# Causal mask moved from TensorE's decay products to the products of C and B, and part of the step's small work moved to GpSimd

## The chip, the cores and the metric

One core of a Trainium2 chip runs the whole program in one launch. The metric is the device time of the program in microseconds (us). Engines are named as the profile names them: PE is TensorE, DVE is VectorE, ACT is ScalarE, POOL is GpSimd, SP is SyncE, which here only issues DMA transfers.

## The reference

The input is 8 sequences of 512 tokens with 128 features. A layer norm with modulation is followed by four Mamba-2 layers, a gated residual, a second modulated norm and a feed-forward block with a shared expert and top-2 routing over 8 experts. The change touches only the Mamba-2 layers:

```python
zxbcdt = h @ Wi                                   # z 256, x 256, B 128, C 128, dt 8
xBC = silu(cb + causal 4-tap convolution of xBC)
dt  = softplus(dt + dtb);  A = -exp(Alog);  dA = exp(dt * A)
hs  = hs * dA_t + (dt_t * x_t) * B_t              # state, 8 heads x 32 x 128
y_t = hs @ C_t  + D * x_t
y   = rmsnorm(y * silu(z)) @ Wo
```

## The kernel before

Features lie on partitions and tokens along the free dimension. The recurrence is computed in chunks of 128 tokens, four to a sequence. Within a chunk the output at token t is the sum over s ≤ t of (C_t·B_s) exp(cum_t − cum_s) dt_s x_s, where `cum` is the running sum of dt·A, which is negative. So each chunk needs the 128x128 products of B and C (`bank[5]`, all four chunks side by side), and for each of the 8 heads a 128x128 matrix of decays, with s on partitions and t along the free dimension. For s > t the exponent is positive and the entry has to become zero.

One step handles one sequence of one layer: 32 steps. The steps are software-pipelined over three steps: the body of step k does part A of step k (projection, convolution, step size), part B of step k−1 (decays, products, state) and part C of step k−2 (norm and output projection); N marks that step k+1 exists. The middle steps are a hardware loop. Every engine has its own program order, written out by hand, and all ordering between engines is by counting semaphores. A wait holds all that stands behind it on that engine.

Names that the prediction uses:
- `tap(t, s)` on DVE: the four taps of the convolution of feature block t (0 and 1 are x, 2 is B, 3 is C). `tap(0, 0)` opens the step on DVE. The blocks are read straight from PSUM banks 0 and 1, so `project(t)` on PE, which fills bank t mod 2, waits for the last tap of block t−2. `project(4)` and `project(5)` make z.
- `decays(n)` on PE, n = 0 to 3: two banks (2 and 3) of four heads each, for a pair of chunks. For each bank there is a mask matmul (identity x mask, 128 rows, 512 columns), one matmul with `PC` as weights and the negative selection `nselb` moving (32 rows, 512 columns), which gives −cum_s, and four of 128 columns with `selb` as weights and `PC` moving, which give +cum_t, the positive half. That is 12 matmuls per call and 48 per step.
- `decay_exp(i)` on ACT: E = exp of a decay bank, i = 0 to 7. `apply_decay(i)` on DVE: M = E x products of C and B, written M0 to M7 in the prediction. `within(c)` on PE: the 8 heads of chunk c, needs M of its chunk. M5 overwrites a tile that `within(1)` reads, and so waits for it.
- `softplus` (the tile `dt_`), `running_sum` (`cum`), `decay_to_end` (`wdec`) and `scale_out` (`o_sb`) on DVE. `dA` on ACT is made from `dt_`.
- `p0`, `p1`, `p2` on POOL: `cum` split in three bf16 parts, rows 0 to 23 of each group of 32 partitions (one group for each chunk). SP copies p2 to `PC` (one DMA) and to `P4` (three), which PE reads in the next step.
- `rows_of_heads` on PE and `E2`, `ti` on ACT and DVE: the part of the output that comes from the state before the chunk.
- `ms` in the prediction is the 512-column matmul of `mean128` and `sqh` (line 604). It uses bank 0 again, and waits for ACT to copy z's first half out of it (`zraw`, line 1022). The second half is copied at line 1047. Both go through Silu later in the step, when ACT has loaded the Silu table.

Weights of the feed-forward block are split on POOL and stored by SP during steps 1 to 18; that is the `W` in the bodies of both.

Of the kernel before, what the change touches and what calls it, by code (L numbers as in the profile page):

```python
# [60 lines left out]
def build(nc, x, w_in, w_out, par, cst, c_t, wmod, par2, w1, w2, out):  # L61
    ctx = ExitStack()
    with ctx:
# [323 lines left out]
        def _(pe):  # L387
# [68 lines left out]
            def body(k, A, B, C, N):  # L456
# [1308 lines left out]
```

## Time and profile before

| | us |
|---|---|
| median of 3 runs | 1203.54 (1201.79 to 1203.59) |
| profiled execution | 1201.13 |
| its span in the trace | 1199.3 |
| PE busy | 1056.5 (88%) |
| DVE busy | 1001.3 (83%) |
| ACT busy | 889.5 (74%) |
| POOL busy | 578.0 (48%) |

The profiled execution is 2.4 us below the median of the runs, and 1.8 us longer than its span. The steps of the Mamba-2 layers fill the span from about 31 us to about 850 us. In the middle of it (400 to 700 us) the granted TensorE clock is 1.00, and of 300 us PE is busy 289.71, DVE 270.83, ACT 263.26 and POOL 151.71.

### The profile page before, as it was taken

The page shows a single profiled execution, that of the slowest core. Times are in us where ns is not written, and L with a number is a line of the kernel's source. Part 1 is how long each engine was busy: PE and PEld are TensorE (multiplying, and loading weights), DVE is VectorE, ACT ScalarE, POOL GpSimd, SP SyncE. Part 2 cuts the span into 40 slices and gives each one's busy share as a digit, 9 for nine tenths or more (in the row PEclk, how much of TensorE's full clock was granted, in tenths as well). Part 3 has the DMA queues.
Part 4 walks back from the last instruction along what each step waited for, and adds up shares of the span by engine and source line. Part 5 has one row for each costly group of instructions (what it writes and reads, how often), then busy time and mean ns, then how long its engine had stood idle before and what let it go on. Part 6 is the DMA issues. An engine that isn't in the chain of part 4 may idle for free.

```text
span 1199.3 us, 27505 instructions
## 1 busy us (share of the span) xinstructions
PE 1056.5 (88%) x7160; PEld 603.5 (50%) x7160; DVE 1001.3 (83%) x1864; ACT 889.5 (74%) x1724; POOL 578.0 (48%) x721
## 2 busy tenths in 40 slices
PE   5699999999999999999999999997688876999980
PEld 4245544455445554455445554444344444777760
DVE  6798999999998999888998899885578875888865
ACT  5688888888888888888888888886466543565540
POOL 0254566446654566435543455434245451566661
PEclk9899999999999999999999999999789987999995
DMA  4111422233222322210000100000010014776737
GB/s 137 36 34 34 144 91 83 83 115 122 84 85 85 136 98 85 75 29 23 22 22 24 29 19 24 22 16 1 3 33 32 27 36 142 233 227 219 233 117 210
DMA packets 85581, 98.08 MB, mean 82 GB/s; under 512 B 20698, under 2 KB 65888, under 8 KB 85536
## 3 DMA queue, kind: packets, MB, share of 16 engines
q1 hardware_dynamic: 80544, 89.08, 23.5%
q0 software_dynamic: 4992, 8.48, 2.1%
q8 instruction: 18, 0.29, 0.1%
q14 instruction: 27, 0.22, 0.1%
HBM read 59.67 MB, written 37.83 MB: 81 GB/s over the span
## 4 chain that ended last, share of the span: by engine, by line
PE 53%; DVE 20%; issue 13%; ACT 8%; DVEq 2%; DMA 1%; POOL 1%; SPq 1%; ACTq 0%; POOLq 0%
PE bank L475 8%; PE bank L548 5%; ACT xbc L1062 4%; DVE cv L1331 4%; PE bank L604 3%; PE bank L522 3%; PE bank L667 3%; DVE cv L1327 3%; PE bank L484 2%; PE bank L485 2%; PE bank L492 2%; PE bank L491 2%; DVE stmp L1434 2%; DVE M L1341 2%; PE bank L668 2%
## 5 line engine op out<-in xcount | busy, mean ns | idle before, releaser
L1331 DVE SCALAR_TENSOR_TENSOR cv<-bank,PAR,cv 128x511 f32<-128x511 f32 (+2 forms) x384 | 273.8, 740 | 9.1 <-DVE cv L1327 4.2
L1637 POOL TENSOR_TENSOR yt<-yt,ti 128x384 f32<-128x384 f32 x64 | 64.2, 1004 | 331.0 <-DVE ti L1453 331.0
L1341 DVE TENSOR_TENSOR M<-E,bank 128x512 f32<-128x512 f32 x256 | 170.6, 677 | 38.8 <-PE bank L548 30.9
L929 ACT ACTIVATE E<-bank 128x512 f32<-128x512 f32 x256 | 148.6, 594 | 28.1 <-DVE M L1341 27.6
L475 PE MATMUL bank<-hn,WA 128*128 128x512 f32 x256 | 144.6, 647 | 21.0 <-DVE cv L1331 20.6
L1668 POOL DMA_INDIRECT RS<-y,XR x92 | 99.6, 1083 | 78.1 <-DVE y L1546 56.4
L1079 ACT ACTIVATE hr<-bank,W1B 128x512 f32<-128x512 f32 x92 | 63.3, 688 | 57.1 <-PE bank L669 53.4
L1661 POOL DMA_INDIRECT XS<-stage,IDX x64 | 64.5, 1008 | 79.5 <-DVE run L1306 55.7
L1062 ACT ACTIVATE xbc<-cv 128x512 f32<-128x512 f32 x128 | 77.0, 626 | 21.7 <-DVE yt L1448 20.5
L1641 POOL TENSOR_TENSOR y<-yt,zs 128x512 f32<-128x512 f32 x64 | 81.3, 1271 | 20.6 <-POOL yt L1637 19.9
L548 PE MATMUL bank<-M,dtx 128*32 128x128 f32 x2048 | 82.5, 278 | 9.9 <-DVE M L1341 7.3
L1476 DVE TENSOR_TENSOR hL<-hr,hH 128x512 fp32r<-128x512 f32 x124 | 87.2, 703 | 4.3
L1601 POOL TENSOR_TENSOR dtx<-xtok,DTW 128x256 f32<-128x256 f32 x128 | 82.0, 641 | 16.8 <-ACT xtok L949 16.8
L522 PE MATMUL bank<-maskb,idb 128*128 128x512 bf16 x256 | 81.3, 383 | 1.7 <-DMA P<-p 1.7
L548 PEld LDWEIGHTS bank<-M,dtx 128*32 128x32 f32 x2048 | 49.1, 109 | 55.1 <-issue 50.6
L1474 DVE CAST hH<-hr 128x512 fp32r<-128x512 f32 x124 | 54.1, 436 | 25.2 <-ACT hr L1079 22.5
L475 PEld LDWEIGHTS bank<-hn,WA 128*128 128x128 f32 x256 | 39.1, 191 | 65.4 <-issue 46.7
L653 PE MATMUL bank<-hn,WA 128*128 128x512 f32 x128 | 63.4, 618 | 0.6 <-ACT DTW L1051 0.6
L1327 DVE TENSOR_SCALAR cv<-bank,PAR 128x512 f32<-128x512 f32 x64 | 51.6, 806 | 13.6 <-ACT xbc L1062 13.5
L1606 POOL TENSOR_TENSOR xw<-xtok,DTW 128x256 f32<-128x256 f32 x96 | 60.6, 631 | 0.0
L644 PEld LDWEIGHTS bank<-xbc,S 128*128 128x128 f32 x384 | 47.6, 192 | 17.8 <-DVE S L1440 13.6
L508 PE MATMUL bank<-CST,xbc 128*128 128x128 f32 x384 | 54.2, 277 | 2.3 <-ACT u L958 0.5
(242 smaller groups left out, 2657.5 us busy)
## 6 DMA issues: line engine op xcount, KB each, us to landing
XS<-PADT SPq DMA_DIRECT2D x32, 520.0 KB, 4.0
WA<-w_in SPq DMA_DIRECT2D x192, 64.0 KB, 1.8
W1B<-WD SPq DMA_DIRECT2D x23, 514.0 KB, 3.5
W2B<-WD SPq DMA_DIRECT2D x23, 512.5 KB, 4.9
WD<-WS SPq DMA_DIRECT2D x16, 512.0 KB, 2.7
XR<-XS SPq DMA_DIRECT2D x23, 260.0 KB, 4.4
RW<-w_in SPq DMA_DIRECT2D x18, 256.0 KB, 4.3
WO_raw<-w_out SPq DMA_DIRECT2D x32, 128.0 KB, 3.5
```

The costliest lines, as they stand in the source:

```text
L475: mm(bank[t % 2][:, :], WA[t][:, :], hn[:, :], start=True, stop=True).then_inc(pj_mm, 1)
L522: mm(bank[2 + b][:, :].rearrange("p (n t) -> p n t", n=4), idb[:, :], maskb[:, :].unsqueeze(1).to_broadcast([P, 4, P]), start=True, stop=F ...
L548: ins = mm(bank[6 + hh // 4][q:q + 32, c * CH:(c + 1) * CH], dtx[c][:, hh * HD:(hh + 1) * HD], M[2 * (hh // 4) + c % 2][:, (hh % 4) * CH:( ...
L929: f(E[i % 2][:, :], bank[2 + i % 2][:, :], ACT.Exp).then_inc(e_a, 1)
L1062: f(xbc[t][:, :], cv[t][:, :], ACT.Silu).then_inc(silu_a, 1)
L1327: ts(cv[t][:, :], src[:, :], PAR[:, bass.ds(cw + 3, 1)], PAR[:, bass.ds(pk + C_CB + t, 1)], ALU.mult, ALU.add).then_inc(tap_v[t], 1)
L1331: stt(out=cv[t][:, s:L], in0=src[:, 0:L - s], scalar=PAR[:, bass.ds(cw + 3 - s, 1)], in1=cv[t][:, s:L], op0=ALU.mult, op1=ALU.add).then_in ...
L1341: tt(M[i % 4][:, :].rearrange("p (n t) -> p n t", n=4), E[i % 2][:, :].rearrange("p (n t) -> p n t", n=4), bank[5][:, c * CH:(c + 1) * CH] ...
L1476: tt(hL[t][:, :], hr[t][:, :], hH[t][:, :].bitcast(F32), ALU.subtract).then_inc(hl_v, 1)
L1601: tt(dtx[c][:, :].rearrange("p (h d) -> p h d", h=NH), xv, DTW[:, 32 * c:32 * c + NH].unsqueeze(2).to_broadcast([P, NH, HD]), ALU.mult).th ...
L1641: tt(y2[t][:, :], yt[t][:, :], zs[:, bass.ds((j % 2) * 2 * L + t * L, L)], ALU.mult).then_inc(fin_p, 1)
L1668: nc.gpsimd.indirect_dma_start(RS[:, :], bass.IndirectOffsetOnAxis(ap=XR[i % XD][:, (c + 1) * ROW - 1:(c + 1) * ROW].bitcast(I32), axis=0) ...
```

## The change

1. `decays(n)` loses the mask matmul. Rows 24 to 31 of each group of 32, which were empty, now carry a coarse mask: in `PC` row 24 + b is one for the tokens of the b-th block of 16, and in `nselb` it is −1e30 for the columns of all earlier blocks of 16. They are made once at the start, from an iota on POOL. So the matmul with `nselb` also sends whole blocks before the token's own to −1e30, and only inside the 16x16 blocks on the diagonal positive exponents are left. SP must not write over these rows: it copies 24 rows of each group in four DMAs, where it copied 128 rows in one.
2. The four 128-column matmuls with `selb` as weights are replaced by one matmul of 512 columns for each bank: weights are ones (32 rows), the moving operand is `own`, a block-diagonal copy of p2 (p2 x `selb`, 128x1024 bf16) that POOL makes in two instructions. So `decays(n)` has 4 matmuls of 512 columns, 16 per step.
3. On DVE a new instruction `causal_products` multiplies the four chunks of products in `bank[5]` by a 0/1 table in place (PSUM in, PSUM out). M0 waits for it. `apply_decay` becomes min(E, 1) x products in one scalar_tensor_tensor with an immediate.
4. `dt_` and `wdec` move from DVE to POOL: `dt_` is the first thing of POOL's body, `wdec` stands behind p2.
5. ACT no longer copies z's second half. Its Silu reads bank 1 directly, and stands first after the Silu table load; `project_early(k + 1, 1)` on PE waits for it in place of the copy.

```diff
-SILU_TURN = [3, 4, 0, 5]
+SILU_TURN = [3, 4, 1, 5]
@@ SP
-                    sp.dma_start(PC[:, :], p2[:, :]).then_inc(p4_in, 16)
+                    if not B:
+                        wait(sp, const_v, 10)
+                    for c in range(NC):
+                        q = 32 * c
+                        sp.dma_start(PC[q:q + 24, :], p2[q:q + 24, :]).then_inc(p4_in, 16)
@@ PE, decays(n)
-                                wait(pe, p4_in, 64 * (j + 1))
+                                wait(pe, p4_in, 112 * (j + 1))
                             wait(pe, fin_v, 4 * j - 1 + b)
-                        mm(bank[2 + b][:, :].rearrange("p (n t) -> p n t", n=4), idb[:, :],
-                           maskb[:, :].unsqueeze(1).to_broadcast([P, 4, P]), start=True, stop=False)
+                        q = 32 * (pair + b)
+                        mm(bank[2 + b][:, :], PC[q:q + 32, :], nselb[q:q + 32, g * 512:(g + 1) * 512],
+                           start=True, stop=False, tile_position=(q, 0))
                     for b in range(2):
                         q = 32 * (pair + b)
-                        mm(bank[2 + b][:, :], PC[q:q + 32, :], nselb[q:q + 32, g * 512:(g + 1) * 512],
-                           start=False, stop=False, tile_position=(q, 0))
-                    for n4 in range(4):
-                        hh = 4 * g + n4
-                        for b in range(2):
-                            q = 32 * (pair + b)
-                            ins = mm(bank[2 + b][:, n4 * P:(n4 + 1) * P], selb[q:q + 32, hh * P:(hh + 1) * P],
-                                     PC[q:q + 32, :], start=False, stop=(n4 == 3), tile_position=(q, 0))
-                            if n4 == 3:
-                                ins.then_inc(d_mm, 1)
+                        if n == 0 and b == 0:
+                            wait(pe, own_p, 2 * (j + 1))
+                        mm(bank[2 + b][:, :], onesb[q:q + 32, :], own[q:q + 32, g * 512:(g + 1) * 512],
+                           start=False, stop=True, tile_position=(q, 0)).then_inc(d_mm, 1)
@@ PE, before the early projection of the next step's second block
-                    wait(pe, zc_a, 2 * k + 2)
+                    wait(pe, silu_a, 6 * k + 1)
@@ ACT
-                    wait(act, dtc_v, 4 * k + 1)
+                    wait(act, step_p, 2 * k + 1)
                     f(dA[:, :], dt_[:, :], ACT.Copy, scale=PAR[:, bass.ds(pk + C_NA, 1)]).then_inc(da_a, 1)
...
-                    wait(act, pj_mm, 6 * k + 6)
-                    f(zraw[1][:, :], bank[1][:, :], ACT.Copy).then_inc(zc_a, 1)
...
+                    wait(act, pj_mm, 6 * k + 6)
+                    wait(act, fin_p, 4 * (k - 1))
+                    f(zs[:, bass.ds((k % 2) * 2 * L + L, L)], bank[1][:, :], ACT.Silu).then_inc(silu_a, 1)
                     silu(TB)
@@ DVE
+                def causal_products():
+
+                    g = bank[5][:, :].rearrange("p (c t) -> p c t", c=NC)
+                    wait(dve, g_mm, j + 1)
+                    tt(g, g, causal[:, :].unsqueeze(1).to_broadcast([P, NC, CH]), ALU.mult).then_inc(g_v, 1)
+
...
-                        wait(dve, g_mm, j + 1)
+                        wait(dve, g_v, j + 1)
                     wait(dve, y_mm, 4 * j + c - 1)
-                    tt(M[i % 4][:, :].rearrange("p (n t) -> p n t", n=4),
-                       E[i % 2][:, :].rearrange("p (n t) -> p n t", n=4),
-                       bank[5][:, c * CH:(c + 1) * CH].unsqueeze(1).to_broadcast([P, 4, CH]),
-                       ALU.mult).then_inc(m_v, 1)
+                    stt(out=M[i % 4][:, :].rearrange("p (n t) -> p n t", n=4),
+                        in0=E[i % 2][:, :].rearrange("p (n t) -> p n t", n=4), scalar=1.0,
+                        in1=bank[5][:, c * CH:(c + 1) * CH].unsqueeze(1).to_broadcast([P, 4, CH]),
+                        op0=ALU.min, op1=ALU.mult).then_inc(m_v, 1)
@@ DVE, once at the start
+            dve.wait_ge(below_p, NC)
+            ts(ex[:, :], u[:, :], 0.0, -1e30, ALU.is_lt, ALU.mult).then_inc(const_v, 1)
+            dve.wait_ge(const_v, 7)
+            stt(out=nselb[:, :].rearrange("p (h t) -> p h t", h=NH), in0=CST[:, K_SEL:K_SEL + 1024].rearrange("p (h t) -> p h t", h=NH),
+                scalar=-1.0, in1=ex[:, :].unsqueeze(1).to_broadcast([P, NH, P]), op0=ALU.mult, op1=ALU.add).then_inc(const_v, 1)
+            ts(PC[:, :], u[:, :], 0.0, None, ALU.is_equal).then_inc(const_v, 1)
@@ POOL
+                if A:
+                    wait(pool, dta_a, 5 * k + 3)
+                    wait(pool, tr_mm, k)
+                    tt(dt_[:, :], u[:, :], ln1[:, :], ALU.add).then_inc(step_p, 1)
...
+                    wait(pool, dta_a, 5 * k + 4)
+                    tt(wdec[:, :], dt_[:, :], ecs[:, :], ALU.mult).then_inc(step_p, 1)
+                def own_rows(g):
+
+                    if B:
+                        wait(pool, d_mm, 8 * k)
+                    wait(pool, part_p, 4 * k + 4)
+                    tt(own[:, g * 512:(g + 1) * 512].rearrange("p (h t) -> p h t", h=4), p2[:, :].unsqueeze(1).to_broadcast([P, 4, CH]),
+                       selb[:, g * 512:(g + 1) * 512].rearrange("p (h t) -> p h t", h=4), ALU.mult).then_inc(own_p, 1)
```

On DVE, in the loop body, the stretch from the last taps of the first blocks to the running sum (`L1327`, `L1331` taps; `L1351` is `dt_`; `M` is a call of `apply_decay`) reads before:

```order
L1331 SCALAR_TENSOR_TENSOR cv<-bank,PAR,cv 128x510
L58 ISA
L58 ISA [waits g_mm,e_a]
L1341 TENSOR_TENSOR M<-E,bank 128x512 [waits y_mm]
L58 ISA
L1351 TENSOR_TENSOR dt_<-u,ln 128x128 [waits tr_mm,dta_a]
L58 REGISTER_ALU
L1341 TENSOR_TENSOR M<-E,bank 128x512 [waits y_mm,e_a]
L1331 ISA [waits tap1_v]
L1331 SCALAR_TENSOR_TENSOR cv<-bank,PAR,cv 128x509
L58 REGISTER_ALU
L1355 SCALAR_TENSOR_TENSOR cum<-ones_row,dA 128x128 [waits da_a]
```

and now (`L1338` is `causal_products`, `L1347` is `apply_decay`):

```order
L1331 ISA [waits tap1_v]
L1331 SCALAR_TENSOR_TENSOR cv<-bank,PAR,cv 128x510
L1338 TENSOR_TENSOR bank<-bank,causal 128x512 [waits g_mm]
L58 ISA
L58 ISA [waits g_v,e_a]
L1347 SCALAR_TENSOR_TENSOR M<-E,bank 128x512 [waits y_mm]
L58 REGISTER_ALU
L1347 SCALAR_TENSOR_TENSOR M<-E,bank 128x512 [waits y_mm,e_a]
L1331 ISA [waits tap1_v]
L1331 SCALAR_TENSOR_TENSOR cv<-bank,PAR,cv 128x509
L58 REGISTER_ALU
L1356 SCALAR_TENSOR_TENSOR cum<-ones_row,dA 128x128 [waits da_a]
```

The causal product stands in front of M0, and `dt_` between M0 and M1 is gone. `wdec`, further down in front of `spend`, is gone too.

On PE, `decays(3)` and what stands behind it reads before (`L604` is `ms`, `L548` is `within(1)`):

```order
L575 MATMUL bank<-P,selxb 128x384 [waits e2_a]
L58 REGISTER_ALU
L522 MATMUL bank<-maskb,idb 128x512 [waits e_a]
L58 REGISTER_ALU
L522 MATMUL bank<-maskb,idb 128x512 [waits e_a]
L526 MATMUL bank<-nselb,PC 128x512 x2
L532 MATMUL bank<-PC,selb 128x128 x8
L58 REGISTER_ALU
L58 ISA [waits sqh_a]
L604 MATMUL bank<-sqh,mean 128x512 [waits zc_a]
L58 REGISTER_ALU [waits m_v]
L548 MATMUL bank<-M,dtx 32x128 [waits px_p]
```

and now (`L529` is `nselb`, `L535` is `own`, `L605` is `ms`):

```order
L576 MATMUL bank<-P,selxb 128x384 [waits e2_a]
L58 REGISTER_ALU
L529 MATMUL bank<-nselb,PC 128x512 [waits e_a]
L58 REGISTER_ALU
L529 MATMUL bank<-nselb,PC 128x512 [waits e_a]
L535 MATMUL bank<-own,onesb 128x512 x2
L58 REGISTER_ALU
L605 MATMUL bank<-sqh,mean 128x512 [waits zc_a,sqh_a]
L58 REGISTER_ALU [waits m_v]
L549 MATMUL bank<-M,dtx 32x128 [waits px_p]
```

Twelve matmuls are now four, with the same waits ahead of them.

On SP, the end of the step's transfers reads before (`L319` is `PC`, `L321` is `P4`):

```order
L58 ISA [waits d_mm]
L319 DMA PC<-p 128x128 [waits part_p]
L321 DMA P<-p 32x128 x3
L58 REGISTER_ALU
L325 ISA [waits split_p]
L325 DMA WD<-WS 128x1024
```

and now:

```order
L58 ISA [waits d_mm]
L325 DMA PC<-p 24x128 [waits part_p]
L325 DMA PC<-p 24x128 x3
L327 DMA P<-p 32x128 x3
L58 REGISTER_ALU
L331 ISA [waits split_p]
L331 DMA WD<-WS 128x1024
```

Three DMA issues more stand ahead of the three to `P4` and of all later ones.

## Rows read from the trace of the kernel before

**Rows 1.** Waits, 100 to 800 us: engine, line <- releaser: total us, times, longest.

```profile
ACT dA L983 <- DVE dt_ L1351: 25.8, 29, 1.0
DVE M L1341 <- PE bank L548: 25.1, 28, 1.1
```

**Rows 2.** Timeline of DVE: start, us, engine, line, operation, tiles, count, [idle before].

```profile
419.28 0.75 DVE L1331 SCALAR_TENSOR_TENSOR cv<-bank,PAR,cv 128x511 f32<-128x511 f32 x1 [0.15 <-DVE cv L1327]
...
420.67 2.71 DVE L1331 SCALAR_TENSOR_TENSOR cv<-bank,PAR,cv 128x510 f32<-128x510 f32 x4
...
423.89 0.61 DVE L1351 TENSOR_TENSOR dt_<-u,ln 128x128 f32<-128x128 f32 x1
424.42 0.67 DVE L1341 TENSOR_TENSOR M<-E,bank 128x512 f32<-128x512 f32 x1
425.02 0.73 DVE L1331 SCALAR_TENSOR_TENSOR cv<-bank,PAR,cv 128x509 f32<-128x509 f32 x1
...
428.95 0.69 DVE L1369 TENSOR_TENSOR o_sb<-bank,rY 128x512 f32<-128x512 f32 x1
429.55 2.29 DVE L1331 SCALAR_TENSOR_TENSOR cv<-bank,PAR,cv 128x509 f32<-128x509 f32 x3
...
434.58 2.10 DVE L1341 TENSOR_TENSOR M<-E,bank 128x512 f32<-128x512 f32 x3 [0.70 <-PE bank L548]
...
448.48 0.62 DVE L1351 TENSOR_TENSOR dt_<-u,ln 128x128 f32<-128x128 f32 x1
```

**Rows 3.** Timeline of PE in the same step.

```profile
425.90 1.10 PE L475 MATMUL bank<-hn,WA 128*128 128x512 f32 x2
...
430.44 1.10 PE L475 MATMUL bank<-hn,WA 128*128 128x512 f32 x2
...
438.63 1.98 PE L653 MATMUL bank<-hn,WA 128*128 128x512 f32 x4
...
442.25 0.75 PE L522 MATMUL bank<-maskb,idb 128*128 128x512 bf16 x2
```

**Rows 4.** Timeline of PE, decays(3) between its neighbours.

```profile
431.73 0.60 PE L522 MATMUL bank<-maskb,idb 128*128 128x512 bf16 x2
432.27 0.39 PE L526 MATMUL bank<-nselb,PC 32*128 32x512 bf16 x2
432.50 0.39 PE L532 MATMUL bank<-PC,selb 32*128 32x128 bf16 x8
432.81 0.70 PE L604 MATMUL bank<-sqh,mean 128*128 128x512 f32 x1
```

**Rows 5.** Timeline of ACT in the same step.

```profile
431.57 0.60 ACT L1022 ACTIVATE zraw<-bank 128x512 f32<-128x512 f32 x1 [0.33 <-PE bank L475]
...
437.28 1.28 ACT L1062 ACT_TABLE_LOAD   x1
```

**Rows 6.** Groups by line and form: operation, tiles, shapes, count, busy us, mean ns.

```profile
L1341 DVE TENSOR_TENSOR M<-E,bank 128x512 f32<-128x512 f32 x256 | 170.6, 677 | 38.8 <-PE bank L548 30.9 <-PE bank L559 2.4 <-ACT E L929 1.5
...
L1331 DVE SCALAR_TENSOR_TENSOR cv<-bank,PAR,cv 128x511 f32<-128x511 f32 x128 | 95.0, 742 | 4.8 <-DVE cv L1327 4.2 <-ACT cv L941 0.2
```

**Rows 7.** The same for two small DVE forms.

```profile
L1522 DVE TENSOR_TENSOR st<-tile_no,st 128x23 f32<-128x23 f32 x1 | 0.2, 183 | 0.0
L1524 DVE SCALAR_TENSOR_TENSOR row_f<-ee,st 128x23 f32<-128x23 f32 x1 | 0.2, 183 | 0.0
```

**Rows 8.** The same for POOL.

```profile
L1628 POOL TENSOR_TENSOR WS<-RW,WS 128x512 fp32r<-128x512 f32 x16 | 20.5, 1280 | 1.3
...
L1614 POOL TENSOR_TENSOR r<-cum,p 128x128 f32<-128x128 f32 x32 | 13.7, 427 | 2.5
```

**Rows 9.** Timeline of SP, DMA issues at the end of the step.

```profile
436.28 0.53 SPq L319 DMA_DIRECT2D PC<-p  x1
436.85 1.86 SPq L321 DMA_DIRECT2D P<-p  x3
```

**Rows 10.** DMA issues by line: KB each, median us from issue to landing.

```profile
P<-p SPq DMA_DIRECT2D x96, 8.0 KB, 1.7
```

More of the change, by code:

```diff
@@ L83, in build @@
         mean256 = sb("mean256", P)
-        idb, onesb = sb("idb", P, BF16), sb("onesb", P, BF16)
-        maskb = sb("maskb", P, BF16)
+        onesb = sb("onesb", P, BF16)
+        causal = sb("causal", P)
         selb = sb("selb", 1024, BF16)
@@ L116, in build @@
         nselb = sb("nselb", 1024, BF16)
+        own = sb("own", 1024, BF16)
         WA = [sb(f"WA{t}", P) for t in range(6)]
@@ L122, in build @@
         xbc = [sb(f"xbc{t}", L) for t in range(4)]
-        zraw = [sb(f"zraw{t}", L) for t in range(2)]
+        zraw = sb("zraw", 2 * L)[:, 0:L]
         u, ax, ex, ln1 = sb("u", P), sb("ax", P), sb("ex", P), sb("ln1", P)
@@ L602, in body @@
                     wait(pe, sqh_a, k + 2)
-                    wait(pe, zc_a, 2 * k + 1)
+                    wait(pe, zc_a, k + 1)
                     mm(bank[0][:, :], mean128[:, :], sqh[:, :], start=True, stop=True).then_inc(ms_mm, 1)
                 elif A:
-                    wait(pe, zc_a, 2 * k + 1)
+                    wait(pe, zc_a, k + 1)
                     square_mean_of_h(0)
@@ L611, in body @@
                     project(5)
-                    wait(pe, dtc_v, 4 * k + 4)
+                    wait(pe, dtc_v, 2 * k + 2)
+                    wait(pe, step_p, 2 * k + 2)
                     if N:
@@ L1004, in body @@
                 if A:
-                    wait(act, dtc_v, 4 * k + 2)
+                    wait(act, dtc_v, 2 * k + 1)
                     f(ecs[:, :], cum[:, :], ACT.Exp, scale=-1.0, bias=cum[:, CH - 1:CH]).then_inc(dta_a, 1)
@@ L1021, in body @@
                     wait(act, pj_mm, 6 * k + 5)
-                    f(zraw[0][:, :], bank[0][:, :], ACT.Copy).then_inc(zc_a, 1)
+                    f(zraw[:, :], bank[0][:, :], ACT.Copy).then_inc(zc_a, 1)
                 if B:
@@ L1062, in silu @@
                         f(xbc[t][:, :], cv[t][:, :], ACT.Silu).then_inc(silu_a, 1)
+                    wait(act, pj_mm, 6 * k + 6)
+                    wait(act, fin_p, 4 * (k - 1))
+                    f(zs[:, bass.ds((k % 2) * 2 * L + L, L)], bank[1][:, :], ACT.Silu).then_inc(silu_a, 1)
                     silu(TB)
-                    for t in range(2):
-                        if t == 0:
-                            wait(act, zc_a, 2 * k + 2)
-                        wait(act, fin_p, 4 * (k - 1))
-                        f(zs[:, bass.ds((k % 2) * 2 * L + t * L, L)], zraw[t][:, :], ACT.Silu).then_inc(silu_a, 1)
+                    wait(act, zc_a, k + 1)
+                    f(zs[:, bass.ds((k % 2) * 2 * L, L)], zraw[:, :], ACT.Silu).then_inc(silu_a, 1)
                     silu(X0)
@@ L1355, in running_sum @@
                     nc.vector.tensor_tensor_scan(cum[:, :], ones_row[:, :], dA[:, :], 0.0, ALU.mult, ALU.add).then_inc(dtc_v, 1)
-                def decay_to_end():
-                    wait(dve, dta_a, 5 * k + 4)
-                    tt(wdec[:, :], dt_[:, :], ecs[:, :], ALU.mult).then_inc(dtc_v, 1)
                 def chunk_decay():
@@ L1463, in _ @@
             dve.wait_ge(s_cst, 16)
[L1464 to L1465 removed]
+            ts(causal[:, :], CST[:, K_MASK:K_MASK + P], 0.0, None, ALU.is_ge).then_inc(const_v, 1)
             cp(selb[:, :], CST[:, K_SEL:K_SEL + 1024]).then_inc(const_v, 1)
[L1467 removed]
+            dve.wait_ge(below_p, NC)
[4 more added lines that the diff above has]
+            ts(PC[:, :], u[:, :], 0.0, None, ALU.is_equal).then_inc(const_v, 1)
             cp(selxb[:, :], CST[:, K_SELX:K_SELX + 256]).then_inc(const_v, 1)
@@ L1586, in _ @@
             tt = nc.gpsimd.tensor_tensor
+            for c in range(NC):
+                nc.gpsimd.iota(u[32 * c:32 * c + 32, :], pattern=[[1, 8], [0, 16]], base=24, channel_multiplier=-1,
+                               allow_small_or_imprecise_dtypes=True).then_inc(below_p, 1)
+                pool.wait_ge(below_p, c + 1)
             nc.gpsimd.memset(PADT[:, :], 0.0).then_inc(padt_p, 1)
@@ L1609, in body @@
                 if A:
-                    wait(pool, dtc_v, 4 * k + 2)
+                    wait(pool, dtc_v, 2 * k + 1)
                     tt(p0[:, :], cum[:, :], CST[:, K_M1:K_M1 + 1].to_broadcast([P, CH]), ALU.mult).then_inc(part_p, 1)
@@ L1632, in body @@
                     tt(hb, hb, o_sb[:, :], ALU.add).then_inc(hup, 1)
+                if A:
+                    own_rows(0)
+                    own_rows(1)
                 if B:
@@ L1638, in body @@
                         wait(pool, fin_p, 4 * j + 1 + 2 * t)
-                        wait(pool, silu_a, 6 * j + 2 + t)
+                        wait(pool, silu_a, 6 * j + 3)
                         wait(pool, out_mm, j)
```

18 lines of the change are left out of this document (5 added, 13 removed).

## The prediction, made before the changed kernel was run

> **What bounds the kernel now.** The table of busy times comes first: PE 88%, DVE 83%, ACT 74%, and none of them at its limit. In such a kernel a saving counts only if it lies on the path through the step, so the rest is read from one step of the loop. The waits of the middle of the run come second [rows 1]: 28 times, once a step, M5 on DVE waits for `within(1)` on PE, 25.1 us in all, 0.90 us a time; ACT's `dA` waits for `dt_`, 25.8 us in 29 times, 0.89 us a time. Third, the timelines. The period is 448.48 − 423.89 = 24.59 us [rows 2], and 30 steps run at it.
>
> Which of PE and DVE leads changes within a step. From M5 (434.58) through the state update to the fourth of the first taps (420.67 in the next step, that is 445.26) DVE works without a gap that another engine causes. After that the two hand over to each other. `tap(1, 3)` starts at 425.02 and lasts 0.73; `project(3)` starts on PE at 425.90 [rows 2, 3]. The output projection behind it ends just before `o_sb`, 428.95. `tap(2, 3)` starts at 429.55, 0.74 us for one of the three, and ends at 430.29 by that; `project(4)` starts at 430.44 [rows 2, 3]. Then PE alone: `rows_of_heads`, `decays(3)` 431.73 to 432.81, `ms`, `within(1)`, and M5 starts when it ends [rows 4, 2]. So of the four calls of `decays`, only the one behind `project(4)` is on the path. The others end before a DVE result that PE needs anyway.
>
> **decays(n) on PE.** From the start of the mask pair to `ms` it takes 432.81 − 431.73 = 1.08: the mask pair 0.54, the `nselb` pair 0.23, the eight small ones with what follows 0.31 [rows 4]. A single `nselb` matmul of 512 columns would take about half the mask pair's time, so the two with different row groups run side by side. The new call is two such pairs, 2 x 0.23, and a tail of 0.10 (0.31 less four overlapped pairs of 128 columns at a quarter of 0.21): 0.56, or 0.67 if the first pair also pays the 0.11 by which the mask pair exceeds two times 0.215. I take 0.60 and a saving of 0.48; bounds are 0.41 and 0.54, and zero if the pairs did not overlap (4 x 0.27 = 1.08). Times four that is 1.9 us of PE a step, of which 0.48 is on the path.
>
> **The causal product on DVE.** The trace has no DVE instruction that writes PSUM. The nearest rows are M, 677 ns for 512 elements with one PSUM input, and the tap, 742 ns [rows 6]; a write to PSUM could cost something more, and from below the spacing of back-to-back M is 0.60. I take 0.69, between the two rows and like `o_sb` [rows 2]. M0 reads its result, and such a wait between neighbours on DVE costs 0.15 beyond the end of the first [first of rows 2]. So M0 starts 0.84 later. `dt_` gives back its spacing, 424.42 − 423.89 = 0.53 [rows 2]. Everything from `tap(1, 3)` on is 0.31 later on DVE.
>
> **apply_decay with a clamp.** Does scalar_tensor_tensor cost the 65 ns more that separate the tap from M [rows 6]? The tap has a pointer to a scalar in SBUF; the clamp's scalar is an immediate. Two small forms tell them apart: 183 ns for tensor_tensor and 183 ns for scalar_tensor_tensor with an immediate at 23 elements [rows 7]. I take nothing; the other bound is 8 x 0.065 = 0.52 a step, of which four stand ahead of `o_sb`.
>
> **dt_ and wdec to POOL.** A 128x128 tensor_tensor of POOL is 427 ns [rows 8]. `dt_` comes before `dtx`, at once after the last product of the step before, and is ready for `dA` by about 1.0 us earlier; ACT's wait of 0.89 goes. ACT then runs into its next wait: E2 needs M0, which is later by 0.84. So the ACT gain is spent before it reaches `cum` or the output norm, and I count it as nothing. `wdec` stands behind p2 and is needed some 5 us later. Off DVE it leaves only more idle time before M5, since M5 waits for PE.
>
> At 128x128 `dt_` is 0.61 on DVE [rows 2], much more than 128 elements explain. The Trainium skill (SBUF — State Buffer, "Who interferes with whom") says that a VectorE instruction with two SBUF inputs contends with a GpSimd instruction that reads SBUF, and one with at most one SBUF input does not. By that rule the causal product, with one input in PSUM, pays no such price although POOL works beside it. If it paid what `dt_` pays over the 0.23 or so that its size asks for, 0.38, the gain per step would be gone; no row here shows a multiply into PSUM beside POOL.
>
> **own on POOL.** Two instructions of 128x512 with two inputs, 1.28 each at most by the nearest row [rows 8], 2.6 together. They wait for the last decays of the step (432.5), and in steps with weights at most one instruction of that size, the addition to `h`, may still stand before them then: they end by 436.5. PE needs them at 441.9, and POOL had nothing to do from that addition to `ti`. They cost nothing, and would not at twice the price. The Trainium skill (GPSIMD Engine Reference, "3. Performance versus the Vector engine") has GpSimd at about half of VectorE's rate for two inputs and keeps elementwise work on VectorE; the rate agrees with the row (1280 ns against 692 for `o_sb`), and the rule would speak against the change only if POOL were on the path.
>
> **PC in four transfers.** An issue on SP takes 0.53 and 0.62 [rows 9]; three more are 1.9 us. Before, the last of `P4` is issued at 436.85 + 1.24 = 438.09 and lands at 439.8 [rows 9, 10]; PE asks for it in `decays(0)` at 442.25 [rows 3]. Now SP begins 0.33 earlier (below), at 435.95, issues seven at 0.62, the last at 439.67, and it lands at 441.4; PE asks at 441.9. This hides, with 0.5 us to spare, and the `decays(0)` that is shorter by 0.48 gives as much again before PE is late for the transposes behind it. Cost nothing.
>
> **z's second half.** ACT loses a copy of 0.5 us between `rB` and the copy to `DTW`. The table load starts at 437.28 [rows 5], now about 0.8 earlier, and Silu of bank 1 ends near 438.4. PE's early projections start at 438.63 [rows 3] with the other bank first and reach bank 1 near 439.3. The new wait costs nothing in steady state. ACT's Silu of x waits for DVE's `yt` as before, so the earlier table load gains nothing.
>
> **The sum.** `tap(1, 3)` is 0.31 later. `project(3)` had 425.90 − 425.75 = 0.15 in hand, of which some 0.06 is the signal: it moves by 0.23, and `o_sb` behind it. `tap(2, 3)` then ends at 430.52, and `project(4)` starts at 430.58: 0.14 to 0.15 later. `decays(3)` gives 0.48: `ms` at 432.48 in place of 432.81. The other input of `ms` is the `zraw` copy, 431.57 + 0.60 [rows 5], which shifts with `project(4)` to end at 432.32, so `ms` can't be before 432.38. M5 is 0.33 earlier (0.43 at most). From M5 to the next first taps all is as it was. Gain 0.33 a step, or with c for the causal product's duration: 1.02 − c. 30 steps give 9.9 us. Outside them I take 1 us of loss, about half of the three more issues (1.9 us) for which the first `decays(0)`, right behind its transfers, may have to wait. 1201.13 − 9.9 + 1.0 = 1192.2 for the profiled execution, and 2.4 more for the median: **1194.6 us**.
>
> **Rivals.**
> - *More than this.* If the pairs start under `rows_of_heads` and the causal product costs its spacing alone (0.60), the whole wait of M5 comes into reach: 0.5 to 0.9 a step, 1178 to 1190. For: 0.90 of slack on DVE. Against: the copy of `zraw`, which caps `ms`. 0.10.
> - *No change: the clamp at the tap's price.* Four of 65 ns before `o_sb` take 0.26 of the 0.33, and three more behind M5 another 0.13. That leaves −0.06: 1206. Against it stand the equal small forms. At half that price 0.13 a step is left, 1200.6. Together, 1200 to 1206, 0.15.
> - *Slower: the multiply in place.* If reading and writing PSUM take turns, c is twice 0.68, 1.36. 1.02 − c gives −0.34 a step, 1214.7. It decides from c = 0.99, and is a loss of over 2.4 us from 1.07. For: no row excludes it, and DVE leads where it stands. 0.10.
> - *The transfers are late.* With 0.2 us more for each of seven issues `decays(0)` is 0.9 us late, of which 0.48 is covered: 0.42 a step, against 0.33 gained, 1207. For: four of the seven are of a size that the trace does not show. Against: the 0.5 us in hand. 0.05.
> - *Forecast*, 0.60: c from 0.60 to 0.80 and a `decays` saving from 0.41 to 0.54 give 0.15 to 0.42 a step, 1191.6 to 1200.
>
> The range is 1186 to 1204: it adds the part of the first two rivals nearest to the forecast. A change of less than 0.2%, 2.4 us, can't be told from none with this kernel. Faster takes the forecast, the first rival and part of the others: 0.77. Same 0.11, slower 0.12.
>
> **What would show it.** In the changed profile: the causal product in its own group, near 0.69 us; `apply_decay` at 677 ns; `decays(3)` from start to `ms` about 0.6; the wait of M5 for `within(1)` shorter than 0.9 but there; no wait of `dA` for `dt_`; a period of 24.26. PE should wait more, for `tap(1, 3)` and `tap(2, 3)`. Wrong would be: a causal product above 1 us, `decays(0)` waiting for `P<-p` in each step, or M5 without any wait.

## The result, and the profile after

The changed kernel takes 1198.78 us (median of 10 runs, 1196.68 to 1200.79). The kernel before took 1201.41 in its 10 runs beside them (1199.65 to 1203.92). The ratio is 0.9973, 95% interval 0.9963 to 0.9983: 2.6 us or 0.27% faster. The prediction was 1194.6, 8.9 us below the median of before. The direction holds; the gain is three tenths of the one forecast.

The profiled execution took 1199.3, its span 1197.3. Busy time per engine, the first part of the page:

```profile
PE 992.9 (83%) x6136; PEld 560.2 (47%) x6136; DVE 1000.5 (84%) x1833; ACT 870.8 (73%) x1692; POOL 675.6 (56%) x853
```

PE has 63.6 us less work than before and POOL 97.6 more; the time hardly moved. Waits from 100 to 800 us (engine, line <- releaser: total us, times, longest; `...` stands for rows left out):

```profile
PE bank L549 <- DVE o_sb L1366: 15.3, 29, 0.5
...
DVE M L1347 <- PE bank L549: 12.9, 28, 0.8
...
PE bank L605 <- ACT zraw L1024: 6.7, 28, 0.2
...
DVE M L1347 <- DVE bank L1338: 6.0, 28, 0.2
...
PE bank L529 <- DMA P<-p: 5.5, 15, 0.7
```

The wait of M5 is down from 25.1 us [rows 1] to 12.9, and that of `dA` for `dt_` is gone. The first row is new: `within(0)` waits 0.53 us in each step for `o_sb`. The third is the cap by `zraw` that the prediction named.

Groups by line and form (count, busy us, mean ns, idle before):

```profile
L1347 DVE SCALAR_TENSOR_TENSOR M<-E,bank 128x512 f32<-128x512 f32 x256 | 168.4, 679 | 28.5 <-PE bank L549 16.6 <-DVE bank L1338 6.0 <-ACT E L931 1.3
...
L1634 POOL TENSOR_TENSOR own<-p,selb 128x512 bf16<-128x512 bf16 x64 | 72.8, 1161 | 14.6 <-PE bank L535 14.5
...
L1338 DVE TENSOR_TENSOR bank<-bank,causal 128x512 f32<-128x512 f32 x32 | 22.1, 690 | 2.7 <-PE bank L560 2.7
L1360 DVE TENSOR_SCALAR spend<-CST,p 128x32 bf16<-128x32 f32 x32 | 18.4, 577 | 0.0
```

The clamp costs 2 ns on the 677 of M [rows 6]; the causal product takes 0.69 us, as taken. Now one step on DVE, to be laid beside rows 2:

```profile
420.81 0.81 DVE L1327 TENSOR_SCALAR cv<-bank,PAR 128x512 f32<-128x512 f32 x1 [0.37 <-ACT xbc L1062]
...
425.78 0.69 DVE L1338 TENSOR_TENSOR bank<-bank,causal 128x512 f32<-128x512 f32 x1
426.68 1.28 DVE L1347 SCALAR_TENSOR_TENSOR M<-E,bank 128x512 f32<-128x512 f32 x2 [0.21 <-DVE bank L1338]
427.88 0.74 DVE L1331 SCALAR_TENSOR_TENSOR cv<-bank,PAR,cv 128x509 f32<-128x509 f32 x1
...
431.81 0.69 DVE L1366 TENSOR_TENSOR o_sb<-bank,rY 128x512 f32<-128x512 f32 x1 [0.21 <-PE bank L498]
...
434.63 0.85 DVE L1360 TENSOR_SCALAR spend<-CST,p 128x32 bf16<-128x32 f32 x1
...
436.92 2.10 DVE L1347 SCALAR_TENSOR_TENSOR M<-E,bank 128x512 f32<-128x512 f32 x3 [0.19 <-PE bank L549]
...
445.26 0.81 DVE L1327 TENSOR_SCALAR cv<-bank,PAR 128x512 f32<-128x512 f32 x1 [0.37 <-ACT xbc L1062]
```

and the same step on PE, beside rows 3 and 4, then `zraw` on ACT:

```profile
428.77 1.10 PE L481 MATMUL bank<-hn,WA 128*128 128x512 f32 x2 [0.34 <-DVE cv L1331]
...
431.74 0.38 PE L535 MATMUL bank<-own,onesb 32*128 32x512 bf16 x2
432.65 0.65 PE L549 MATMUL bank<-M,dtx 128*32 128x128 f32 x16 [0.53 <-DVE o_sb L1366]
433.31 1.10 PE L481 MATMUL bank<-hn,WA 128*128 128x512 f32 x2
434.33 0.33 PE L576 MATMUL bank<-P,selxb 32*128 32x384 bf16 x1
434.34 0.39 PE L529 MATMUL bank<-nselb,PC 32*128 32x512 bf16 x2
434.56 0.38 PE L535 MATMUL bank<-own,onesb 32*128 32x512 bf16 x2
435.18 1.10 PE L605 MATMUL bank<-sqh,mean 128*128 128x512 f32 x2 [0.24 <-ACT zraw L1024]
436.21 0.65 PE L549 MATMUL bank<-M,dtx 128*32 128x128 f32 x16
```

```profile
434.44 0.60 ACT L1024 ACTIVATE zraw<-bank 128x512 f32<-128x512 f32 x1 [0.66 <-PE bank L481]
```

The period is 445.26 − 420.81 = 24.45 us, and from `hn` to `hn` 24.46 in all steps of the middle, against 24.60 before. To find where the 0.33 went, each step is taken as its distance from the step's first tap. Two rows of before are needed for that, the tap itself and `within(0)`:

```profile
418.32 0.81 DVE L1327 TENSOR_SCALAR cv<-bank,PAR 128x512 f32<-128x512 f32 x1 [0.36 <-ACT xbc L1062]
```

```profile
429.78 0.64 PE L548 MATMUL bank<-M,dtx 128*32 128x128 f32 x16
```

| us after the first tap | before | after | moved | predicted |
|---|---|---|---|---|
| `tap(1, 3)` | 6.70 | 7.07 | +0.37 | +0.31 |
| `project(3)` | 7.58 | 7.96 | +0.38 | +0.23 |
| `o_sb` | 10.63 | 11.00 | +0.37 | +0.23 |
| `within(0)` | 11.46 | 11.84 | +0.38 | not followed |
| `project(4)` | 12.12 | 12.50 | +0.38 | +0.14 |
| `ms` | 14.49 | 14.37 | −0.12 | −0.33 |
| M5 | 16.26 | 16.11 | −0.15 | −0.33 |

From `project(4)` to `ms` the time fell by 0.50, close to the 0.48 of the prediction, though for another reason (the section on the prediction has it). What failed is ahead of it: the loss on DVE reaches `project(4)` whole.

The SP queue at the end of this step, beside rows 9:

```profile
438.67 3.09 SPq L325 DMA_DIRECT2D PC<-p  x4
441.81 1.81 SPq L327 DMA_DIRECT2D P<-p  x3
```

Four copies of 24 rows take 0.77 us each, more than the 0.53 for one of 128 rows.

Outside the steady steps: `hn` of step 2 is at 73.03 us against 68.38, so the start lost 4.65 us; the 29 periods up to step 31 gain 4.24, and the rest gains another 2.4, which leaves the 2.0 of the profiled pair. That rest, from the last `hn` to the end, lasts from 414.6 to 419.1 us in the fourteen traces kept, in no order that follows the changes, so the 2.4 can't be credited to this one. The period is the number to rely on.

### The profile page after: what moved, and what is told of

It reads as the page before. It is cut to its first block and busy times, and to the rows that moved or that the text cites. A ratio compares the mean times of both kernels' runs of the same rounds, so it can differ in the third digit from the quotient of the medians.

```text
span 1197.3 us, 25713 instructions
## 1 busy us (share of the span) xinstructions
PE 992.9 (83%) x6136; PEld 560.2 (47%) x6136; DVE 1000.5 (84%) x1833; ACT 870.8 (73%) x1692; POOL 675.6 (56%) x853
## 5 line engine op out<-in xcount | busy, mean ns | idle before, releaser
L1331 DVE SCALAR_TENSOR_TENSOR cv<-bank,PAR,cv 128x511 f32<-128x511 f32 (+2 forms) x384 | 273.7, 740 | 11.6 <-DVE cv L1327 4.3
L1347 DVE SCALAR_TENSOR_TENSOR M<-E,bank 128x512 f32<-128x512 f32 x256 | 168.4, 679 | 28.5 <-PE bank L549 16.6
L1634 POOL TENSOR_TENSOR own<-p,selb 128x512 bf16<-128x512 bf16 x64 | 72.8, 1161 | 14.6 <-PE bank L535 14.5
L529 PE MATMUL bank<-nselb,PC 32*128 32x512 bf16 x256 | 52.5, 388 | 12.8 <-DMA P<-p 8.7
L1327 DVE TENSOR_SCALAR cv<-bank,PAR 128x512 f32<-128x512 f32 x64 | 51.5, 805 | 13.6 <-ACT xbc L1062 13.5
L514 PEld LDWEIGHTS bank<-CST,xbc 128*128 128x128 f32 x384 | 44.4, 143 | 33.2 <-ACT u L960 16.3
```

The lines of the kernel that those rows point to most:

```text
L514: ins = nc.tensor.transpose(bank[TURN_BANK[c]][:, n * P:(n + 1) * P], xbc[t][:, c * CH:(c + 1) * CH], ident)
L1331: stt(out=cv[t][:, s:L], in0=src[:, 0:L - s], scalar=PAR[:, bass.ds(cw + 3 - s, 1)], in1=cv[t][:, s:L], op0=ALU.mult, op1=ALU.add).then_in ...
L1347: stt(out=M[i % 4][:, :].rearrange("p (n t) -> p n t", n=4), in0=E[i % 2][:, :].rearrange("p (n t) -> p n t", n=4), scalar=1.0, in1=bank[5 ...
```

## The experiments

The periods are distances between `hn` in the middle of each run. Steps 1 to 18 also carry the feed-forward weights; where only these differ, both are given. A time without a range is of a single run, and the readings rest on the periods.

**Without the causal product.** Everything else of the change stays; masking inside the 16x16 diagonal blocks is left out.

```diff
-                        wait(dve, g_v, j + 1)
+                        wait(dve, g_mm, j + 1)
-                    causal_products()
```

> The changed kernel without the causal product; it leaves out the mask inside the 16x16 blocks on the diagonal. Period now 24.46 us. Theory 1 (handover without slack: what DVE is late in front of M0 is paid in full through tap(1,3), project(3), the output projection, o_sb, within(0) and project(4)): 0.90 us leave DVE, of which 0.50 count, since PE's own work ends 0.50 before project(3) starts; period 23.96. Theory 2 (the small gain comes from elsewhere: POOL beside DVE, or transfers that arrive late for decays(0)): 24.3 to 24.46. The prediction's formula, 1.02 - c with some slack, gave 24.46 - 0.75 = 23.7 or less.

1183.09 us, period 23.88, a little below the 23.96 of theory 1. The product costs 0.58 of its 0.90 (0.69 and the wait of 0.21). The remainder is a limit on the other side:

```profile
589.35 0.69 DVE L1366 TENSOR_TENSOR o_sb<-bank,rY 128x512 f32<-128x512 f32 x1 [0.71 <-PE bank L498]
```

DVE has the time, but `o_sb` now waits for PE.

**The positive half by `selb` again, no `own`.**

```diff
-                    for b in range(2):
-                        mm(bank[2 + b][:, :], onesb[q:q + 32, :], own[q:q + 32, g * 512:(g + 1) * 512], ...)
+                    for n4 in range(4):
+                        for b in range(2):
+                            ins = mm(bank[2 + b][:, n4 * P:(n4 + 1) * P], selb[...], PC[q:q + 32, :], ...)
```

> The changed kernel with the positive half made as before, by eight matmuls of 128 columns from selb, and without own on POOL; the coarse mask and the causal product stay. Theory 1 (ms is held by the copy of zraw, 0.24 us behind the end of decays(3)): eight small ones with tail take 0.31 us, the own pair some 0.33, so the period stays at 24.46 (24.42 to 24.50). Theory 2 (own is what shortens decays): +0.1 to +0.3. If POOL's own disturbs DVE in the steps with weights (spend lasts 0.85 us there, 0.23 in the others), those steps get shorter by up to 0.3.

1199.28 us, period 24.47. By itself this period could hide up to 0.24, since `ms` waits that long for `zraw`. The version further down that has neither `own` nor this wait settles it: from `project(4)` to the matmuls behind `decays(3)` it takes 1.57 us (328.28 to 329.85), and 1.57 with `own` as well (573.29 to 574.86). So of the saving in `decays(3)` all comes from the mask pair; the 72.8 us on POOL buy nothing.

**`dt_` and `wdec` back on DVE.**

```diff
+                if A:
+                    softplus()          # after M0, as before
+                    decay_to_end()      # before spend, as before
```

> The changed kernel with dt_ and wdec back on DVE. Theory 1: dt_ adds its 0.53 us in front of tap(1,3), all of it paid: period 24.99; wdec hides in the wait of M5 (0.81 us in the steps without weights). Theory 2 (DVE has slack there): 24.46 to 24.6.

1218.48 us, period 25.08: 0.62 more than the change. From the start of `dt_` to the start of M1 it is 0.61 here (460.47 to 461.08). A whole instruction on DVE is paid in full.

**An own semaphore for `PC`.** `decays(0)` waits for the four `PC` transfers, and `rows_of_heads` for those of `P4`.

```diff
-                        sp.dma_start(PC[q:q + 24, :], p2[q:q + 24, :]).then_inc(p4_in, 16)
+                        sp.dma_start(PC[q:q + 24, :], p2[q:q + 24, :]).then_inc(pc_in, 16)
-                                wait(pe, p4_in, 112 * (j + 1))
+                                wait(pe, pc_in, 64 * (j + 1))
```

> The changed kernel with a semaphore of its own for the four transfers to PC, so that decays(0) no longer waits for the three to P4 behind them; rows_of_heads waits for those. Steady period unchanged by both theories, 24.46 (decays(0) waits 0.37 us in 15 steps, covered). Start: the 4.65 us by which hn of the third step lags the kernel before (73.03 against 68.38) shrink by up to 1.8, the three issues, if theory 1's reading holds that the first decays(0) waits for its transfers; by nothing if the tables made at the start are all of it.

1198.89 us, period 24.46. The DMA waits of the steady steps (5.5 us in 15 steps) cost nothing. In the start `hn` goes from step 1 to step 2 in 23.22 us, against 24.33 with the change and 22.08 before; what of this is the transfers follows in the account of the start.

**One instruction of that size on the kernel before**, ahead of M0, into a scratch tile.

```diff
+                    wait(dve, g_mm, j + 1)
+                    tt(scr[:, :], bank[5][:, :], CST[:, 128:640], ALU.mult).then_inc(scr_v, 1)
```

> The kernel before with one more DVE instruction of the causal product's shape in front of M0 (bank 5 times a constant, written to a scratch tile; nobody waits for it). It adds its spacing, 0.60 us. Theory 1: all of it is paid, period 24.60 + 0.60 = 25.20. The prediction's step (0.15 us in hand at project(3), more at project(4)): 25.05. Theory 2 (M5 waits 0.90 us for PE, DVE has room): 24.6 to 24.7.

1216.61 us, period 25.17, 0.57 more than before; the theory of no slack said 25.20, the prediction's step 25.05.

```profile
408.37 0.68 DVE L1386 TENSOR_TENSOR scr<-bank,CST 128x512 f32<-128x512 f32 x1
408.96 0.67 DVE L1343 TENSOR_TENSOR M<-E,bank 128x512 f32<-128x512 f32 x1
```

The instruction takes 0.59 from start to start. All but 0.02 is in the period. This is the experiment that refutes the slack on its own.

**`dt_` and `wdec` to POOL, nothing else**, on the kernel before.

```diff
 # POOL, first in the body
+                    tt(dt_[:, :], u[:, :], ln1[:, :], ALU.add).then_inc(step_p, 1)
 # POOL, behind p2
+                    tt(wdec[:, :], dt_[:, :], ecs[:, :], ALU.mult).then_inc(step_p, 1)
 # DVE
-                    softplus()
-                    decay_to_end()
```

> The kernel before with only dt_ and wdec moved to POOL. Theory 1: PE's square means end at the moment at which tap(1,3) lets project(3) go, so PE and DVE tie there and 0.53 us less on DVE give nothing: 24.5 to 24.6. Theory 2 (DVE leads there alone): 24.07 to 24.2.

1197.61 us in one run, period 24.40, a shorter one than with the whole change. It gives 0.20 of the 0.53 taken from DVE, and the rest is seen as a wait:

```profile
428.76 0.69 DVE L1370 TENSOR_TENSOR o_sb<-bank,rY 128x512 f32<-128x512 f32 x1 [0.63 <-PE bank L492]
...
434.40 2.10 DVE L1342 TENSOR_TENSOR M<-E,bank 128x512 f32<-128x512 f32 x3 [1.23 <-PE bank L548]
```

So the place is one-sided. DVE later is paid in full; DVE earlier gives 0.20, then PE's own matmuls ahead of `o_sb` are the bound.

**z's second half copied again**, with Silu from the copy.

```diff
+                    f(zraw1, bank[1][:, :], ACT.Copy).then_inc(zc1_a, 1)
-                    wait(pe, silu_a, 6 * k + 1)
+                    wait(pe, zc1_a, k + 1)
```

> The changed kernel with z's second half copied out of PSUM again before DTW, 0.5 us of ACT, and the wait of the early projection on that copy. Theory 1: ACT idles 1.18 us in front of the Silu of x for DVE's yt, and the early projection starts 1.9 us after DTW: period 24.46, unchanged. If ACT's time there counts: up to 24.95.

1198.39 us, period 24.46 or 24.47: the copy was worth nothing either way.

**`within(1)` ahead of `ms` on PE**, on the changed kernel. `ms` waits for `zraw`; `within(1)`, which M5 waits for, does not.

```diff
+                if B:
+                    within(1)
                 if N:
                     ...                 # waits for sqh and zraw, then ms
-                if B:
-                    within(1)
```

> The changed kernel with within(1) in front of ms on PE, so that M5 no longer stands behind the copy of zraw. Theory 1: M5's wait goes; in the steps with weights DVE is busy until 0.2 us before M5, and project(5) is held by tap(3,3), so the period falls by 0.2 to 24.25; in the steps without, by 0.5 to 23.95. Theory 2 (late transfers or POOL hold the step): 24.46.

1187.47 us, period 24.26 with weights and 23.86 without. PE from `project(4)` on, in a step without weights:

```profile
573.29 1.10 PE L481 MATMUL bank<-hn,WA 128*128 128x512 f32 x2
...
574.33 0.39 PE L529 MATMUL bank<-nselb,PC 32*128 32x512 bf16 x2
574.55 0.38 PE L535 MATMUL bank<-own,onesb 32*128 32x512 bf16 x2
574.86 0.64 PE L549 MATMUL bank<-M,dtx 128*32 128x128 f32 x16
575.44 1.13 PE L607 MATMUL bank<-sqh,mean 128*128 128x512 f32 x2
```

No gap is left, and DVE goes from `tap(3, 3)` into M5 and M6; only M7 waits, for its E:

```profile
576.01 1.27 DVE L1347 SCALAR_TENSOR_TENSOR M<-E,bank 128x512 f32<-128x512 f32 x2
577.80 0.69 DVE L1347 SCALAR_TENSOR_TENSOR M<-E,bank 128x512 f32<-128x512 f32 x1 [0.52 <-ACT E L931]
```

**The same, and `tap(3, 3)` ahead of `spend` and M4 on DVE.**

```diff
+                    tap(3, 3)
                     chunk_decay()
                     apply_decay(4)
-                    tap(3, 3)
```

> As the one before, and on DVE tap(3,3) in front of spend and M4. Theory 1: project(5) is let go 0.7 to 1.4 us earlier, and both kinds of step come to 23.9 or 24.0, unless M4, now 0.65 later, holds E6 and with it M6 and within(2); then nothing is gained over the one before. Theory 2: 24.46.

1212.72 us, period 25.02 with weights and 24.76 without, so 0.90 worse than without this move. The tap was to let `project(5)` go earlier. But it stands ahead of M4 now, and the exp of E6 waits for M4:

```profile
616.24 0.81 DVE L1360 TENSOR_SCALAR spend<-CST,p 128x32 bf16<-128x32 f32 x1
616.97 2.09 DVE L1347 SCALAR_TENSOR_TENSOR M<-E,bank 128x512 f32<-128x512 f32 x3
```

```profile
617.75 0.60 ACT L931 ACTIVATE E<-bank 128x512 f32<-128x512 f32 x1 [1.03 <-DVE M L1347]
```

From `o_sb` to M4 it is 616.97 − 612.54 = 4.43 us in place of 574.76 − 571.80 = 2.96 with the swap alone: 0.89 for the tap and 0.58 for a slower `spend` (explained at the end). M4 to M7 shrinks by 0.57. The sum is the 0.90.

**Three versions that build on this**, each timed in 5 rounds against the kernel before, 1201.91 in these rounds.

*Changed kernel, swap, own semaphore for `PC`, and no `own`* (the edits above together):

> The changed kernel with within(1) in front of ms, with the eight small matmuls in place of own, and with the own semaphore for PC. Period 23.86 in steps without weights, as with the exchange alone, since eight small matmuls take what the own pair takes (0.31 us); in steps with weights at most 24.26, and less if POOL's own was what made spend long there. With the earlier first decays(0) the total should be 1184 to 1187, 1.2% below the kernel before. Were own what shortens decays on the path, the period would be 24.1.

1185.22 us (1183.81 to 1186.85), ratio 0.9859 (0.984 to 0.9879); period 24.34 with weights, 23.87 without. The 24.34 is 0.08 above what was expected: `spend` takes 0.93 us here, and 0.85 with the swap alone.

*Changed kernel, swap, own semaphore, `tap(2, 3)` ahead of `o_sb` and `project(4)` ahead of `within(0)`*:

```diff
+                    tap(2, 3)
                     scale_out()
-                    tap(2, 3)
-                    within(0)
                     ...                 # project(4)
+                    within(0)
```

> The changed kernel with within(1) in front of ms, and with tap(2,3) in front of o_sb on DVE and project(4) in front of within(0) on PE, so that project(4) no longer stands behind the wait of within(0) for o_sb (0.53 us a step); own semaphore for PC. Theory 1: PE comes to decays(3) 0.25 us earlier; period 23.65 to 23.86 without weights. If DVE, without a gap there, leads instead, nothing is gained.

1188.12 us (1186.6 to 1189.3), ratio 0.988 (0.9861 to 0.99); period 24.34 and 23.78. It gave nothing beyond the swap where weights are carried, because after the swap DVE is the bound there. In the version above, in a step with weights:

```profile
326.79 0.69 DVE L1369 TENSOR_TENSOR o_sb<-bank,rY 128x512 f32<-128x512 f32 x1 [0.21 <-PE bank L498]
327.39 2.29 DVE L1334 SCALAR_TENSOR_TENSOR cv<-bank,PAR,cv 128x509 f32<-128x509 f32 x3
329.60 0.93 DVE L1363 TENSOR_SCALAR spend<-CST,p 128x32 bf16<-128x32 f32 x1
330.45 0.68 DVE L1350 SCALAR_TENSOR_TENSOR M<-E,bank 128x512 f32<-128x512 f32 x1
331.04 0.73 DVE L1334 SCALAR_TENSOR_TENSOR cv<-bank,PAR,cv 128x509 f32<-128x509 f32 x1
331.70 2.08 DVE L1350 SCALAR_TENSOR_TENSOR M<-E,bank 128x512 f32<-128x512 f32 x3
```

From `o_sb` to M7 DVE does not wait once.

*Kernel before, `dt_` and `wdec` on POOL, and the swap.* The mask stays on PE:

> The kernel before with only dt_ and wdec on POOL and within(1) in front of ms: no causal product, and the mask in decays as before. It tells what the mask's move is worth once the copy of zraw no longer caps it. decays(3) is 0.5 us longer than in the changed kernel and DVE reaches project(3) some 0.3 earlier: if the first weighs more on the path, period 24.05 to 24.2 (total 1191 to 1195); if not, 23.9.

1185.74 us (1184.42 to 1186.82), ratio 0.9861 (0.9842 to 0.988); period 24.08 in all steps. The period is the expected one, the time is not: 1191 to 1195 was expected, behind the changed kernel with the swap, and the two can't be told apart. Here DVE has 0.90 a step less to do and waits 0.63 at `o_sb` and 0.95 at M7; there PE has less to do. With weights this one has the shorter period, without them the other.

## Why the prediction was partly right

**The causal product (c = 0.69, and the clamp at no price): right.** 690 ns, and 679 against 677. The wait of M0 is 0.21 where 0.15 was taken, so the net on DVE is +0.37, not +0.31. Beside the 128x128 `dt_` the prediction weighed a rule of the Trainium skill (SBUF — State Buffer, "Who interferes with whom"): with one input in PSUM there is no contention with GpSimd. 690 ns with POOL at work agrees: in the step above POOL runs `dtx` and `xw` without a gap from 425.34 on. The 0.23 that the prediction took for the size of `dt_` alone is in no row.

**"`project(3)` had 425.90 − 425.75 = 0.15 in hand, of which some 0.06 is the signal": this is the step that failed.** The 0.15 from the end of `tap(1, 3)` to `project(3)` is the handover itself. After the change it is the same: 428.62 to 428.77. Nothing was in hand. The same holds between `tap(2, 3)` and `project(4)`: 430.29 to 430.44 before, 433.16 to 433.31 after, where the prediction again let lateness shrink. The 0.06 of the wait ahead of M0 and the two slacks of some 0.09 that do not exist turn +0.14 at `project(4)` into +0.38. The extra instruction on the kernel before (+0.57 of 0.59) and `dt_` put back (+0.62) show that DVE's lateness there is paid whole.

The prediction also missed a wait. `within(0)` stands ahead of `project(4)` and needs `o_sb` to have read its bank. Before, `o_sb` ended at 429.64 and `decays(2)` at 429.69, and `within(0)` started at 429.78: a tie that the profile shows as no wait at all. With a shorter `decays(2)` and a later `o_sb` it became the 0.53 in the waits after. That it cost anything is not shown. `within(0)` would let `project(4)` go at 433.31, and so would `tap(2, 3)`, which follows `o_sb` on DVE: 432.42 + 0.74 + 0.15 = 433.31.

**decays(n), saving 0.48: the number is right, by luck.** PE's own work shrank by more. With the swap nothing holds PE behind `decays(3)`, and from `project(4)` to there it takes 1.57 us in place of 432.81 − 430.44 = 2.37. The call itself went from 1.08 to 0.53 (574.33 to 574.86), and it starts 0.25 earlier behind `project(4)`, because its first pair now runs beside the last matmul of `rows_of_heads` (434.34 and 434.33). That is the condition of the rival "more than this". What PE gained beyond 0.50 the `zraw` cap took back. `decays(2)`'s equal saving went into the wait for `o_sb`, as the prediction said of the calls that are not on the path.

**The `zraw` cap: named, but counted as just not binding, and it binds.** From `project(4)` to the start of the copy it is 1.13 us in both kernels, the copy takes 0.60, and `ms` follows its end by 0.14: 1.87, whatever `decays(3)` takes. Before it was 2.37, so 0.50 was all that could be had there. The prediction had 0.06 for this handover too, and so put the cap 0.10 ahead of `ms`. `zraw` moved with `project(4)` by 0.38, and `ms` came 0.12 earlier, M5 0.15. Taking `within(1)` out from behind it was worth 0.60 a step without weights and 0.20 with them.

**The sum.** +0.37 − 0.50 = −0.13 a step against −0.33. (The low end of the forecast, 1191.6, goes with 0.43 a step and not with the 0.42 beside it.) With one rule, DVE's lateness in full, its earliness up to 0.20, and 0.50 for the stretch up to `ms`, the periods of five kernels come out:

| kernel | worked out | measured |
|---|---|---|
| changed | 24.60 + 0.37 − 0.50 = 24.47 | 24.46 |
| no causal product | 24.60 − 0.20 − 0.50 = 23.90 | 23.88 |
| `dt_` and `wdec` back | 24.46 + 0.61 = 25.07 | 25.08 |
| extra instruction on before | 24.60 + 0.59 = 25.19 | 25.17 |
| `dt_` and `wdec` moved on before | 24.60 − 0.20 = 24.40 | 24.40 |

The 0.20 is taken from the last row, and 0.37 and 0.50 are read from the changed kernel, so the first row and the last test nothing. The 0.61 and 0.59 are the times that the added instruction takes from start to start in its own trace. The test is in the three rows between.

**POOL, SP, z: costs of nothing in steady state, right**, though the 0.5 us in hand for the transfers was not there: PE waits some 0.4 for them in 12 steps without weights and 0.2 in three early ones. An issue to `PC` took 0.77 where 0.62 was taken. The own semaphore shows that this wait costs nothing.

**The start, 1 us of loss: too small.** It is 4.65 in the profiled run: `hn` of step 0 is 0.71 later (it lies from 28.44 to 29.64 in the fourteen traces), step 0 takes 1.69 more and step 1 takes 2.25 more. In step 1 PE waits 2.73 us for the transfers ahead of `decays(0)`, where it waited 1.70 before and 0.68 with the own semaphore. Changed kernel, then the one with the own semaphore, each from `decays(0)` to `project(2)`:

```profile
55.44 0.60 PE L529 MATMUL bank<-nselb,PC 32*128 32x512 bf16 x2 [2.73 <-DMA P<-p]
...
61.29 1.49 PE L481 MATMUL bank<-hn,WA 128*128 128x512 f32 x2
```

```profile
52.12 0.39 PE L529 MATMUL bank<-nselb,PC 32*128 32x512 bf16 x2 [0.68 <-DMA PC<-p]
...
56.20 1.12 PE L481 MATMUL bank<-hn,WA 128*128 128x512 f32 x2
```

The same work takes 5.85 us and 4.08. The granted clock of these two stretches is 0.50, the lower level of 1.2 GHz, and 1.00; before the change it is 1.00 from 48 to 76 us. So the start pays for the longer wait, and then for a clock that is at half behind it. With the own semaphore both are gone here, but its clock falls later, to 0.53 from 63 to 68 us, after waits of 1.66 and 0.98 us, and most of the gain is lost again. `hn` of step 2 lies at 69.28 without `own`, 70.62 with the own semaphore, and at 70.71 and 71.10 in the two experiments built on the kernel before, which has 68.38. Kernels whose start is nearly the same differ by some 2 us, and in the first three of these four a stretch at the lower level lies between 48 and 69 us. How the rest divides between the transfers, the clock and other causes is open.

## What to carry to other kernels

A start that follows its releaser's end by 0.15 us had nothing in hand; measure the usual handover first and use it at every crossing, at a cap as well. Before a saving is counted, look for releasers that tie with it, since a tie shows no wait. Where two engines hand over in turn, price earliness and lateness apart: here 0.20 at most for the one, all of it for the other. And when the saving lands in front of a matmul that waits for something else, move the matmul that the next engine needs ahead of it: that one move took the time from 1198.8 to 1187.5 (one run), four times what the change itself had brought.

## What was not expected of the hardware

A small `tensor_scalar` on DVE was held until a POOL instruction ended. `spend` takes 0.23 us where POOL is idle, and 0.85 in the step above, 434.63 to 435.48. POOL's addition to `h` runs at the same time, and ends at 435.45:

```profile
434.18 1.27 POOL L1649 TENSOR_TENSOR h<-h,o_sb 128x512 f32 x1
```

In the experiment with `tap(3, 3)` moved it is 616.24 to 617.05, beside two `own` instructions of 2.27 together from 615.86, of which the first ends at about 617.0. Before the change its mean was 232 ns, after it 577. Without `own` it is still 570, so it is the addition to `h` that holds it in the steps with weights. The Trainium skill (SBUF — State Buffer, "Who interferes with whom") has the pair of ports shared by both engines as a lock held for the whole instruction, which `tensor_scalar` can ask for; the ends of these rows agree. In the version whose DVE is full it is 0.70 a step.

A DVE multiply that reads and writes PSUM takes 690 ns at 128x512, and one from PSUM to SBUF 682 (the extra instruction on the kernel before). On POOL the bf16 product of that size takes 1161 ns against 1280 for the float32 subtraction [rows 8]. An issue on SP costs 0.77 us for 24 rows, 0.60 for 32 and 0.53 for 128: more rows did not take longer.
